# Two engine no-ops behind every indirect gather on GpSimd in a graph network layer

## What is computed

```python
h = jnp.maximum(_layernorm(x, axis=-1), 0.0)
msg_in = jnp.concatenate([h[src], h[dst], edge_attr_32], axis=-1)
messages = swish(msg_in @ W1 + b1) @ W2 + b2
att = softmax(swish(msg_in @ Wa1 + ba1) @ Wa2 + ba2, axis=0)
aggregated = segment_sum(messages * att, dst, num_segments=6250)
out = x + swish(concatenate([h, aggregated], -1) @ Wu1 + bu1) @ Wu2 + bu2
```

## Time and profile before

| | |
|---|---|
| median of 3 runs | 2449.22 us (2447.33 to 2454.1) |
| span of the profiled execution | 2482.0 us |
| PE matmul busy | 1101.1 us, 44% |
| PE weight load busy | 963.4 us, 39% |
| DVE busy | 1086.6 us, 44% |
| ACT busy | 919.5 us, 37% |
| POOL busy | 1529.9 us, 62% |
| mean granted TensorE clock | 0.668 |

### The profile page before, as it was taken

The page is one execution under the profiler, slowest core; times in us unless marked ns, Lnnn a source line. Parts: engine busy times, 40 slices in busy tenths (PEclk is TensorE's granted clock), DMA queues, the critical chain, the costliest instruction groups (busy, mean ns, idle before and its releaser), DMA issues.

```text
span 2482.0 us, 21022 instructions
## 1 busy us (share of the span) xinstructions
PE 1101.1 (44%) x6767; PEld 963.4 (39%) x6767; DVE 1086.6 (44%) x2367; ACT 919.5 (37%) x1107; POOL 1529.9 (62%) x1628
## 2 busy tenths in 40 slices
PE   4334444444444444444444444444444444444447
PEld 3223343444333333444333334343433333444444
DVE  4344444444444444444444444444444444444445
ACT  3333333334333333334333333343433333333433
POOL 4666666666666666666666666666666666666650
PEclk8566666666666666666666666666666666666766
DMA  7433333333333333333333333333333333333321
GB/s 202 106 90 90 90 89 88 92 91 95 98 93 88 90 88 88 90 93 90 99 95 89 89 90 89 87 94 89 98 95 91 89 90 90 87 93 90 95 65 27
DMA packets 101990, 228.43 MB, mean 92 GB/s; under 512 B 45184, under 2 KB 65460, under 8 KB 91636
## 3 DMA queue, kind: packets, MB, share of 16 engines
q1 hardware_dynamic: 47588, 120.63, 18.5%
q0 software_dynamic: 51584, 105.75, 17.2%
q10 hardware_dynamic: 2704, 0.66, 0.1%
HBM read 218.91 MB, written 8.00 MB: 91 GB/s over the span
## 4 chain that ended last, share of the span: by engine, by line
issue 48%; PE 33%; DVE 9%; another core or an unknown queue 7%; ACT 1%; SPq 1%; DVEq 0%; DMA 0%; ACTq 0%
PE bank L622 20%; PE bank L636 11%; DVE hot L865 2%; DVE v L902 2%; DVE bank L912 1%; DVE prod L895 1%; PE bank L732 1%; PE bank L722 0%; DVE lgb L921 0%; DVEq L875 0%; ACT comb L492 0%; PE bank L584 0%; ACT s L524 0%; PE bank L655 0%
## 5 line engine op out<-in xcount | busy, mean ns | idle before, releaser
L404 POOL DMA_INDIRECT p_rows<-p_tab,src_all x1612 | 1521.9, 944 | 872.3 <-issue 464.7
L622 PE MATMUL bank<-q_win,comb 128*128 128x128 f32 x3224 | 723.7, 369 | 981.9 <-issue 963.8
L622 PEld LDWEIGHTS bank<-q_win,comb 128*128 128x128 f32 x3224 | 643.9, 279 | 1099.1 <-issue 1095.4
L492 ACT ACTIVATE comb<-dst_b,row_of 96x1024 f32<-96x1024 int32 (+1 forms) x162 | 219.0, 1352 | 1336.6 <-PE bank L622 1227.8
L911 DVE TENSOR_TENSOR bank<-bank,p_rows 128x128 f32<-128x128 f32 x80 | 23.9, 299 | 1205.5 <-remote 672.6
L636 PE MATMUL bank<-hot,v 128*65 128x96 f32 x3200 | 320.1, 252 | 344.7 <-issue 274.8
L636 PEld LDWEIGHTS bank<-hot,v 128*65 128x65 f32 x3200 | 282.7, 141 | 342.1 <-issue 264.5
L912 DVE TENSOR_TENSOR bank<-bank,p_rows 128x512 f32<-128x512 f32 (+1 forms) x403 | 266.5, 666 | 71.7 <-PE bank L622 38.6
L524 ACT ACTIVATE s<-bank 128x512 f32<-128x512 f32 x403 | 232.1, 589 | 108.7 <-DVE bank L912 83.8
L498 ACT ACTIVATE comb<-comb,ones 96x1024 f32<-96x1024 f32 (+1 forms) x162 | 218.9, 1351 | 2.7
L865 DVE TENSOR_TENSOR hot<-bank,rel 128x960 f32<-128x960 f32 x162 | 178.3, 1139 | 0.0
(11 more groups left out here) (108 smaller groups left out, 304.0 us busy)
## 6 DMA issues: line engine op xcount, KB each, us to landing
dst_b<-dst_row SPq DMA_DIRECT2D x80, 960.0 KB
p_rows<-p_tab,src_all POOLq DMA_INDIRECT x1612
comb<-efT SPq DMA_DIRECT2D x80, 320.0 KB
q_win<-q_tab SPq DMA_DIRECT2D x81, 48.0 KB
p_tab<-s SPq DMA_DIRECT2D x12, 256.0 KB
q_tab<-s SPq DMA_DIRECT2D x12, 256.0 KB
out<-s SPq DMA_DIRECT2D x6, 256.0 KB, 2.3
x_sb<-x SPq DMA_DIRECT2D x2, 512.0 KB, 5.1
```

Of the source, the lines that this page charges most:

```text
L404: pool.indirect_dma_start(p_rows[:, a, t * H2:(t + 1) * H2], None, p_tab, bass.IndirectOffsetOnAxis(src_all[:, g * TG + t:g * TG + t + 1], ...
L492: nc.scalar.activation(comb[0:WIN, a, c0:c1], dst_b[:, c0:c1], ACT.Abs, bias=row_of[0:WIN, bass.ds(g, 1)]).then_inc(abs_ok, 1)
L622: last = nc.tensor.matmul(ps_z[q][:, (t % TQ) * H2:(t % TQ + 1) * H2], comb[:, a, t * P:(t + 1) * P], q_win[:, a, :], start=True, stop=True)
```

## The change

```diff
                         pool.indirect_dma_start(p_rows[:, a, t * H2:(t + 1) * H2], None, p_tab,
                                                 bass.IndirectOffsetOnAxis(src_all[:, g * TG + t:g * TG + t + 1], 0)).then_inc(gath[a][q], 16)
+                        pool.engine_nop()
+                        pool.engine_nop()
             groups(pool, gather)
```

## The result

| | before | with the change |
|---|---|---|
| median | 2451.66 us (2447.33 to 2454.8, 4 runs) | 2463.94 us (2457.46 to 2467.38, 4 runs) |
| ratio | 1 | 1.0046, 95% interval 1.0025 to 1.0067 |

The kernel is slower by 12 us, half a per cent, which lies clear of the noise. The forecast was 106 us.

The account below looks back on a forecast made before the run. POOL's gathers were thought to wait in a loop for PE, let go only after each gather run. With all no-ops on the path, 2449 + 106 = 2555 us was forecast, range 2220 to 2680 us.

Parts of the forecast that it names:

- The side: Whole kernel: slower by the no-ops' own time, chance 0.46; slower in all 0.48, faster 0.40, same 0.12.
- The bound before: Each group: 20 gathers, some 4.8 us until PE is let go and L911 starts, 0.57 us until POOL resumes; 29.43 us.
- The price of a no-op: POOL, behind each gather: 0.033 us each, 0.066 us a gather, 106 us in all.
- the prediction's lower bound, with its condition: Gap between gathers: no-ops cost nothing if two fit into 0.30 us, only if that gap is the sequencer's preparation.
- the neighbouring memset: A one-column memset follows its neighbour after 0.03 us; taken as the nearest row for a no-op's price.
- The place on the path: POOL's wait for L911: a run 1.3 us longer lets PE go 1.3 us later, so no-ops are on the path in full.
- the forecast's rule: End of each gather run: PE is let go and L911 starts some 4.8 us behind the start of the last gather.
- The backlog absorbs it: PE's `zmm` of q3: spacing stays below 1.34 us, only POOL's pause shrinks by 1.3 us; 2449 us, chance 0.12.
- PE is freed: `zmm` of q3 behind `sums`: gathers beyond 1.34 to 1.44 us apart build no backlog, POOL never waits; chance 0.40.
- The gain it promised: Whole kernel with PE freed: a plain row of gathers, 2207 to 2423 us.
- A dear no-op: POOL: each no-op waits for the gather and pays the 0.30 us gap, 967 us more, 3416 us; chance 0.02.

Follow-up runs that it names:

- e13: The change itself (two no-ops behind each gather) against the kernel before, on an occasion where PE is not held up: 2107.24 against 2105.27 us, 0.999.
- e1: The kernel before, unchanged, timed against itself on an occasion where PE is not held up: 2107.47 us, ratio 1.000.
- e2: Eight no-ops behind each gather against the kernel before, PE not held up: 2262.85 us, 1.0748.
- e11: Twelve no-ops behind each gather against the kernel before, PE not held up: 2418.51 us, 1.1481.
- e7: Sixteen no-ops behind each gather against the kernel before, on an occasion where that kernel's PE is held up: 2563.12 us, 1.0449.
- e8: Eight no-ops behind every fourth gather against the kernel before, PE held up: 2463.36 us, 1.0038.
- e6: Four no-ops behind each gather against the kernel before, PE held up: 2461.25 us, 1.0023.
- e18: Twelve no-ops behind each gather against the kernel before, on an occasion where that kernel's PE is held up: 2541.91 against 2486.95 us, 1.0227.

## Why the side was right and the size wrong

**The side: luck.** Slower was forecast for the time of the no-ops, and that time is nothing. Where no pause could hide them the ratio is 0.999 (e13), and what makes the 12 us is open.

**The bound before: right in its parts, wrong in its cause.** POOL waits for PE, which waits for nothing that has a name, and without that the kernel is a plain row of gathers; 1611 steps and two ends of 46 and 48 us are exactly what e1 shows. The forecast took L911 to wait until PE had worked through its slow records. After the change those of q3 are started 6 to 19 us before L913, and it is PE's report that comes late. Already in the rows of before, 10 of the 40 records between two `sums` stand ahead of 1050.53, so the 8 of q3 are among them. The eighth is this one, and L911 comes at 1052.19:

```profile
1046.31 0.37 PE L622 MATMUL bank<-q_win,comb 128*128 128x128 f32 x1 [1.75 <-issue]
```

That the trickle belongs to the chip or the occasion, and that the same program runs in 2106 us on four others, no row of one trace could tell.

**The price of a no-op: the sum's first term failed.** "I take that: 0.033 us each, 0.066 us a gather, ... 106 us in all." The duration was right (37 and 32 ns in the records), the cost was not. Where POOL's row is the whole time, two no-ops cost nothing (e13). Eight, twelve and sixteen cost 0.0207 us each past the third (e2, e11, e7), where 0.033 was forecast from the first on. The gap of 0.30 us has room for the first ones; the prediction's lower bound, with its condition, was the answer, and it chose the neighbouring memset instead. GPSIMD Engine Reference, section "Instruction dispatch", of the Trainium skill led to 0.02 to 0.08 us a no-op: the 0.0207 us agrees with its lower end, and only from the fourth on is it paid. Perfetto Trace Analysis, section "GPSIMD Engine Instruction", of the Trainium skill says to time from start to start; here that is what separates 32 ns on record from 20.7 ns paid.

**The place on the path: failed as well.** "It has followed the end of the gather run by nearly the same time in a run of 20 and at the end of the program." That was one run length seen twice. With other lengths, which the change's own pauses make, PE reports `sums` 28.4 us behind the start of the run, whether the last gather starts 4.4 or 2.8 us ahead (e8 agrees; e6, with pauses all over its runs, does not keep to 28.4 us). The prediction had this number in its rivals (28.86 / 20 = 1.44 us a gather), and gave 0.12 to the one in which POOL's pause shrinks. The run of 40 gathers could have told the two apart: its tail was 2 us longer, where the forecast's rule wanted it unchanged, and from its first gather at 40.0 to L912 at 96.55 are 56.6 us, 1.41 us for each of the 40.

**The rivals.** "The backlog absorbs it" comes nearest, and by both of its ways: the no-ops themselves fit into the gap (e13), and the pauses that POOL has besides are taken out of its wait, 134 us more on one line, 138 us less on the other, the time 0.3 to 0.5% off. PE is freed by gathers that are far enough apart, at 1.431 us (e18) and 1.514 us (e7), where the rival put the point at 1.34 to 1.44 us. The gain it promised did not come: with PE free POOL has pauses of its own (e18), and steps of 1.51 us are longer than those of 1.45 us that the pauses made before. The two ends of a kernel with PE free are 44 to 48 us each (e1, e7, e18), where the rival had 40 and 80. A dear no-op is ruled out.

**What stays open.** The remaining 12 us (first occasion) and 7 us (third). They are there with PE held up (intervals from 1.0025 and 1.0021), and not without it (0.999, interval 0.9971 to 1.0009). Four no-ops, and eight in every fourth place, cost 6 and 8 us like two, so it does not go by their number or by their spacing. POOL's short steps are also lengthened in 200 or so places just ahead of its wait, by 123 us, which the wait gives back almost whole; whether the few microseconds are the rest of that is only argued, since a trace of before with an ordinary span is missing. For the same reason the sums of 134 and 138 us compare traces whose spans differ by 26 us. Nor is it shown what holds PE's reports back, or that gathers and PE share a resource at all: that is a reading of the 28.4 us. It is only shown that neither the clock nor the no-ops make it, and that PE goes on in single records in a window in which no DMA moves a byte.

## What to carry to other kernels

The gap between two instructions of an engine is not all cost: put something small in it where the engine is the bound and see how much is free, before you price an addition by its duration. When a wait ends "a fixed time behind" something, look for a second length of that thing in the trace before building a sum on it; beginning and end of a run can't be told apart while all runs are alike. When an engine waits for matmuls, compare their records with the event that reports them: the two lay 20 us apart here. And time the kernel on more than one chip and occasion before explaining a stall: here a stall worth 345 us was there on three of seven.

## What had not been expected of the hardware

- The same program takes 2106, 2109, 2105 and 2110 us on four occasions and 2452, 2455 and 2487 us on three. The difference is PE. Where it is held up, from some 10 us behind the start of a run of gathers, its instructions start 0.7 us or a multiple of it apart (weights and matmuls in the trace of before at 1034.27, 1034.97, 1035.70, 1037.12, 1037.84, 1038.55), and its report of a finished `sums` comes 18 to 20 us late in the trace after, 0.01 us in e1. POOL's usual step is 1.249 to 1.252 us on both kinds.
- With PE held up, it is let go 28.4 us behind the start of a run of 20 gathers with two no-ops and with eight at every fourth, whatever the run's length inside that time, but not with four. With all three a gather takes 1.452 to 1.453 us in the mean.
- An indirect gather of 128 rows of 512 bytes costs GpSimd 1.249 us when they stand in a row, one of 64 rows 1.207 us.
- Two engine no-ops behind a gather are free, four cost 0.019 us together, and each further one up to sixteen 0.0207 us. With twelve or sixteen, 19 steps of the kernel are longer by about 1 us more, one in every fourth group.
